# A macaron layer on one core: the order of TensorE's work within a quarter of a head pair, and transposes in tiles of 64

## The reference, cut to what matters

```python
x = x + 0.5 * ffn(layernorm(x))
x = x + attn(layernorm(x))      # 16 heads of 64; inside: softmax(q k^T / 8) v, w_proj, + bias + x, layernorm
x = x + 0.5 * ffn(layernorm(x))

def fp4_linear(x, w):           # blocks of 16 rounded to an FP4 grid, scaled by the block's maximum
    return einsum('bsk,nk->bsn', fp4_quant_dequant(x), fp4_quant_dequant(w))
# ffn: silu(fp4_linear(x, w_gate)) * fp4_linear(x, w_up), then fp4_linear(., w_down); inner width 352
```

## Time and profile before

| | us |
|---|---|
| median of three runs | 2568.18 |
| lowest and highest | 2564.86, 2571.95 |
| the profiled execution's own time | 2570.78 |
| its span, first to last instruction | 2569.0 |
| PE busy | 2312.5 (90%) |
| DVE busy | 1721.6 (67%) |
| POOL busy | 1412.9 (55%) |
| ACT busy | 1202.1 (47%) |

### The profile page before, as it was taken

The page is one execution under the profiler, slowest core; times in us unless marked ns, Lnnn a source line. Parts: engine busy times, 40 slices in busy tenths (PEclk is TensorE's granted clock), DMA queues, the critical chain, the costliest instruction groups (busy, mean ns, idle before and its releaser), DMA issues.

```text
span 2569.0 us, 45690 instructions
## 1 busy us (share of the span) xinstructions
PE 2312.5 (90%) x16292; PEld 1220.1 (47%) x16292; DVE 1721.6 (67%) x2830; ACT 1202.1 (47%) x1813; POOL 1412.9 (55%) x1323
## 2 busy tenths in 40 slices
PE   3799899999999999999989998999999999999984
PEld 1344444545454454545444454454545455454542
DVE  4465677767677776767667676776767677765643
ACT  1345454545545454544545444454454545444431
POOL 2255555656556565556556555565655656555551
PEclk7799999999999999999999999999999999999985
DMA  1000000000000000000000000000000000000000
GB/s 49 5 6 2 3 5 6 6 2 10 3 6 6 2 10 2 10 2 6 6 3 10 2 10 3 6 6 2 10 3 6 6 2 10 2 6 2 6 2 9
DMA packets 167394, 16.40 MB, mean 6 GB/s; under 512 B 148160, under 2 KB 166784, under 8 KB 167168
## 3 DMA queue, kind: packets, MB, share of 16 engines
q1 hardware_dynamic: 167168, 13.39, 4.5%
HBM read 7.03 MB, written 4.19 MB: 4 GB/s over the span
## 4 chain that ended last, share of the span: by engine, by line
PE 67%; DVE 20%; issue 6%; ACT 6%; POOL 1%; DVEq 0%; DMA 0%; SPq 0%; ACTq 0%; POOLq 0%
PE pS L943 16%; PE pO L970 12%; PE pM L927 8%; DVE nmax L779 7%; PE pX L991 5%; PE pM L1085 5%; PE pX L955 4%; PE pM L980 3%; PE FpF L284 2%; PE LpF L284 2%; PE FpF L295 2%; PE LpF L256 2%; PE LpF L267 1%; DVE QL L901 1%; PE FpF L256 1%
## 5 line engine op out<-in xcount | busy, mean ns | idle before, releaser
L646 POOL TENSOR_TENSOR ES<-ES,E 128x512 f32<-128x512 f32 x512 | 693.4, 1375 | 265.1 <-ACT E L731 263.5
L779 DVE TENSOR_REDUCE nmax<-pX 128x2 fp32r<-128x1024 f32 x512 | 622.1, 1215 | 161.2 <-PE pX L955 158.3
L731 ACT ACTIVATE E<-pS 128x1024 f32<-128x1024 f32 x512 | 523.2, 1022 | 420.4 <-PE pS L943 408.7
L970 PE MATMUL pO<-E,VA 128*64 128x512 f32 x2048 | 554.6, 620 | 0.0
L640 POOL TENSOR_TENSOR ES<-E 128x512 f32<-128x512 f32 x256 | 320.5, 1274 | 366.0 <-ACT E L731 366.0
L943 PE MATMUL pS<-QH,KH 64*128 64x512 f32 x1024 | 258.7, 501 | 19.6 <-issue 15.1
L927 PE MATMUL pM<-xf,w_raw 128*64 128x512 f32 x1024 | 268.1, 600 | 3.1 <-DVE QL L901 2.4
L741 ACT ACTIVATE KH<-pM 128x512 fp32r<-128x512 f32 x128 | 76.6, 598 | 358.2 <-PE pM L927 358.2
L955 PE MATMUL pX<-KH,QH 64*128 64x512 f32 x1024 | 233.2, 405 | 4.2 <-DVE nmax L779 2.7
L943 PEld LDWEIGHTS pS<-QH,KH 64*128 64x128 f32 x1024 | 96.8, 185 | 285.2 <-issue 253.8
L991 PE MATMUL pX<-wp,ON 128*64 128x128 f32 x2048 | 141.6, 280 | 98.9 <-DVE nmax L779 79.3
(11 more groups left out here) (141 smaller groups left out, 3402.0 us busy)
## 6 DMA issues: line engine op xcount, KB each, us to landing
RROW<-RC SPq DMA_DIRECT2D x512, 2.0 KB, 2.0
xin<-in_L_attn_x SPq DMA_DIRECT2D x16, 256.0 KB, 2.8
SH<-nmax SPq DMA_DIRECT2D x256, 2.0 KB, 2.0
LC<-LROW SPq DMA_DIRECT2D x256, 2.0 KB, 2.1
out<-X SPq DMA_DIRECT2D x16, 256.0 KB, 2.3
w_raw<-in_L_attn_w_q SPq DMA_DIRECT2D x1, 512.0 KB, 4.0
w_raw<-in_L_attn_w_k SPq DMA_DIRECT2D x1, 512.0 KB, 5.6
w_raw<-in_L_attn_w_v SPq DMA_DIRECT2D x1, 512.0 KB, 6.7
```

Source lines behind the costliest of these rows:

```text
L646: ins = g.tensor_tensor(ES[par][:, hd, :], ES[par][:, hd, :], E[s][:, hd, :], ALU.add)
L731: a.activation(E[s][:, :, :], pS[:, :, :], ACT.Exp).then_inc(s_exp, 1)
L779: v.tensor_reduce(nmax[px % 2][:, :, t:t + 1], pX[:, :, :], AX.X, ALU.max, negate=True).then_inc(s_max, 1)
L970: ins = pe_.matmul(pO[half(hd), :], VA[of][:, kt, j * 128 + 64 * hd:j * 128 + 64 * hd + 64], E[kt][:, hd, :], start=kt == 0, stop=kt == KT ...
```

## The change

In PE's walk three things are moved. The product for the maxima comes ahead of the scores in quarters 0, 1 and 3, and stays behind them in quarter 2. The projection goes from before the K product to the end of quarter 1, behind the FFN work; the V product of quarter 3 also goes behind the FFN work. On DVE the sum into Yacc goes behind the remainders QL and KL of its quarter. The last piece of the transposes of h has 64 columns: it starts at column 288 instead of 320, so columns 288 to 319 are turned twice, and the down product takes 128 rows of every chunk. The rows of its weights that meet the doubled columns are zero: w_down's last 32 columns are loaded by a DMA of their own, 32 places on.

```diff
@@ pe_h
-                f0 = ch * 128 + 64 * n
-                w = min(64, FF - f0)
-                ins = self.nc.tensor.matmul(self.pF[64 * n:64 * n + w, ch * 128:(ch + 1) * 128], row[:, f0:f0 + w],
+                f0 = min(ch * 128 + 64 * n, FF - 64)
+                ins = self.nc.tensor.matmul(self.pF[half(n), ch * 128:(ch + 1) * 128], row[:, f0:f0 + 64],
@@ pe_down
-                rows = min(128, FF - ch * 128)
-                                                self.hqT[0:rows, ch, t * 128 + 64 * n:t * 128 + 64 * n + 64],
-                                                self.wdT[0:rows, ch, :], start=ch == 0, stop=ch == FT - 1)
+                                                self.hqT[:, ch, t * 128 + 64 * n:t * 128 + 64 * n + 64],
+                                                self.wdT[:, ch, :], start=ch == 0, stop=ch == FT - 1)
@@ SP, setup (and DVE waits for s_wraw 96 instead of 80)
-                sp.dma_start(wraw[:, 2, 0:FF], w_down).then_inc(s_wraw, 16)
+                sp.dma_start(wraw[:, 2, 0:FF - 32], w_down[:, 0:FF - 32]).then_inc(s_wraw, 16)
+                sp.dma_start(wraw[:, 2, FF:FP], w_down[:, FF - 32:FF]).then_inc(s_wraw, 16)
@@ DVE, body: behind QL (s == 0) and KL (s == 1) instead of ahead of them
+                        if s == 1 and there(i - 3, NP):
...
+                            v.tensor_tensor(Yacc[yp][:, :], pX[:, 0, :], Yacc[yp][:, :], ALU.add).then_inc(s_yacc, 1)
@@ PE, a new helper
+                def max_round(i, p, s):
+                    if s < 2:
+                        for_maxima(i + 1, p + 1, s + 2)
+                    else:
+                        for_maxima(i + 2, p + 2, s - 2)
@@ PE, body
                     for s in range(KT):
+                        if s != 2:
+                            max_round(i, p, s)
                         if there(i, NP):
                             scores(i, p, s)
...
-                        if s < 2:
-                            for_maxima(i + 1, p + 1, s + 2)
-                        else:
-                            for_maxima(i + 2, p + 2, s - 2)
+                        if s == 2:
+                            max_round(i, p, s)
...
-                        if s == 1 and there(i - 3, NP):
-                            project(i, p)
                         if s == 1 and there(i + 2, NP):
                             pe.wait_ge(s_qlo, i + 3)
                             per_head(1, p2, x).then_inc(s_k, 1)
                         if s == 2 and there(i - 1, NP):
                             row_sums(i - 1, 1 - p % 2)
+                        first_ffn(b, 4 * p + s, bpar)
+                        last_ffn(b, 4 * p + s, bpar)
+                        if s == 1 and there(i - 3, NP):
+                            project(i, p)
                         if s == 3:
                             for r in rounds_at(i):
...
-                        first_ffn(b, 4 * p + s, bpar)
-                        last_ffn(b, 4 * p + s, bpar)
```

More of the change, by code:

```diff
@@ L768, in _ @@
                 v.memset(LROW[:, :], 1.0).then_inc(s_ones, 1)
-                dve.wait_ge(s_wraw, 80)
+                dve.wait_ge(s_wraw, 96)
                 F.qh.maxima(nc, dve, 0, F.h[:, 0:NW], slice(0, NW // BLK))
@@ L906, in body @@
                                                    ALU.mult, ALU.subtract).then_inc(s_klo, 1)
+                        if s == 1 and there(i - 3, NP):
+                            bo, yp = (b, bpar) if p >= 3 else (b - 1, 1 - bpar)
+                            dve.wait_ge(s_proj, i - 2)
+                            dve.wait_ge(s_y0, bo + 1)
+                            wait(dve, s_yacc, i - 3)
+                            v.tensor_tensor(Yacc[yp][:, :], pX[:, 0, :], Yacc[yp][:, :], ALU.add).then_inc(s_yacc, 1)
                         first_ffn(b, t, bpar)
```

## The result

The changed kernel took 2473.1 us (median of 4 runs, 2470.86 to 2474.6) against 2566.5 us for the kernel before in the same runs (2560.94 to 2571.95): ratio 0.9635, 95% interval 0.9612 to 0.9659. The forecast was 2473. The profiled execution has a span of 2469.1 us against 2569.0.

A forecast was written before the change was run, and what follows sets the result against it. PE was taken to bound most of a batch, VectorE near it in the third and fifth pair. Terms -116 + 20 - 14 + 10 - 43 + 8 + 46 + 0.5, with clock -6, gave -95 and 2473 us; range 2405 to 2545.

The forecast's parts named there:

- the new waits: Waits added by moving the projection: 12 us for Yacc in quarter 2, 8 us for quarter 3's leading product; 20 us.
- B: V product behind quarter 3's FFN work: -14 us of its wait for ON, +10 us at the next pair's leading product.
- A: Projection last in quarter 1, behind the K product, which covers its wait for VectorE's reduction: -116 us.
- under 20: Sign that the forecast is right: under 20 us of idle time before the projection.
- The 8 us in quarter 3: Quarter 3's leading product waits some 0.5 us for the reduction where VectorE has FFN work behind Yacc, first pair.
- D: Product for the maxima ahead of the scores in quarters 0, 1, 3: strided load exposed, 0.12 us 384 times, +46 us.
- The 35 us that I left in the third pair: V product's wait for ON in the third pair, expected to stay: 15 x 2.3 = 35 us.
- C: Transposes of h in 64-wide pieces: 0.75 instead of 1.09 us, 128 times, -43 us; 8 given back where VectorE paces.
- Rival 4: The strided load of the product for the maxima is hidden in the change of mode: 2427 us, chance 0.12.
- Clock: Steady part: up to 24 us lie in short stretches at 1.2 GHz; with fewer PE waits, -6 us.
- the gate (1): Rival: leading product for the maxima waits for a late reduction and holds up scores behind; slower, chance 0.07.
- VectorE as the bound (2): Rival: VectorE takes over in four pairs, only fourth, sixth, seventh and eighth gain; -53, 2515 us, chance 0.14.

The follow-up runs named there:

- e6: Changed kernel with the projection ahead of the K product again and the sum into Yacc ahead of QL and KL: 2533.3 us, ratio 0.9849.
- e10: Kernel before with only the product for the maxima put ahead of the scores in quarters 0, 1 and 3: 2582.3 us, ratio 1.0054.
- e7: Changed kernel with the V product ahead of the FFN work of quarter 3 again: 2489.7 us, ratio 0.9673 to the kernel before.
- e2: Changed kernel with the scores ahead of the product for the maxima in all four quarters: 2435.7 us, ratio 0.9482 to the kernel before.
- e9: Kernel before with only projection, V product and sum into Yacc moved; scores leading, old 32-wide transposes: 2485.0 us, ratio 0.9676.
- e8: Changed kernel with the 32-wide last transpose piece, 96-row chunk and single w_down load again: 2537.2 us, ratio 0.9855 to the kernel before.
- e1: Kernel before with only the 64-wide transposes, 128-row down product and split weight load: 2558.3 us, ratio 0.9961.
- e3: Changed kernel, product for the maxima loading 128 consecutive QH columns instead of every fourth: 2437.7 us, ratio 0.9489 to the kernel before.
- e4: Changed kernel with VectorE's moments of the layernorm after attention, and GpSimd's root, one quarter later: 2436.5 us, ratio 0.9487 to the kernel before.

## Why the prediction was right

The sum came out at -95 us and the measurement at -94. The mechanisms were the forecast ones, the sizes were not all: the transposes brought 15 us more, the new waits cost about 16 more, the projection gained about 13 less and of the +10 of B only 4 came. That the total is right to 1 us is luck; the terms as the traces have them add up to -84, and 7 us of the rest are waits that the sum did not name: the scores' for the exponentials, 4.5 us before and none after, and the turn of the hardware loop, 15.1 and 12.1.

**A, -116, with +20 of new waits.** Right in kind. The projection's idle fell by 87 us, to 12.3, within the "under 20" that I had asked for, though not to 5; from the starts its loss fell from 119 us, which the sum had right at 121, to 16. A visit now runs as forecast. PE and VectorE in quarter 1 of the sixth pair, against the earlier trace rows:

```profile
1200.81 1.08 PE L976 MATMUL pO<-E,VA 128*64 128x512 f32 x4
1201.72 1.03 PE L926 MATMUL pM<-xf,w_raw 128*64 128x512 f32 x4
1202.58 1.04 PE L997 MATMUL pX<-wp,ON 128*64 128x128 f32 x16
```
```profile
1201.11 1.16 DVE L778 TENSOR_REDUCE nmax<-pX 128x2 fp32r<-128x1024 f32 x1
1203.43 0.69 DVE L898 SCALAR_TENSOR_TENSOR KL<-pM,KH 128x512 fp32r<-128x512 f32 x1 [1.15 <-ACT KH L740]
1204.04 0.68 DVE L905 TENSOR_TENSOR Yacc<-pX,Yacc 128x512 f32<-128x512 f32 x1
```

The next group starts 0.91 after times_v, the K product covers the reduction, and Yacc follows KL. The new wait for Yacc showed itself otherwise than I had put it. It is no idle time of the matmul: the wait sits on its weight load. In quarter 2 of the next visit Yacc ran from 1219.45 for 0.69 us, the load started at 1220.21, and the matmul at 1220.37, half under the scores, half exposed:

```profile
1220.21 0.34 PEld L954 LDWEIGHTS pX<-KH,QH 64*128 64x128 f32 x2
1220.37 0.49 PE L954 MATMUL pX<-KH,QH 64*128 64x512 f32 x2
1220.79 1.08 PE L976 MATMUL pO<-E,VA 128*64 128x512 f32 x4
```

From the starts in the trace, the load begins 0.07 us after the end of Yacc in all of the 123 visits that the trace has whole, and times_v comes late in all of them: by 0.10 us in 76, by 0.20 in 12 and by 0.45 in 35. That is 26 us, nearly all of which no idle column shows. Of the 35, 30 are the fifth and the sixth pair of each batch, two of my three pairs without FFN work in quarter 1, where KL has to be done first; the extra 0.35 us makes 12 us, as forecast. The 0.10 in every visit I had missed. The 8 us in quarter 3 are there too, 0.52 us once a batch, in the fifth pair and not in the first. With 12.3 - 2.7 = 10 us of visible waits for reductions the new waits are some 36, against my 20. A and D were not independent, as e6 and e10 showed: lead and move cover the same 0.48 us. In a sum over the whole change that does no harm; taken one by one my terms would have failed.

**B, -14 and +10.** The forecast net, -4, is too near to e7's 10 for its interval to tell them apart. From the starts V's loss fell from 49 us, as the sum had it, to 39, so 10 instead of 14; and the leading product behind V comes 0.05 to 0.09 us late in 47 visits, 4 us instead of 10. The 35 us that I left in the third pair are there, 35.4 in all pairs together. PE in that pair:

```profile
1155.48 1.08 PE L976 MATMUL pO<-E,VA 128*64 128x512 f32 x4
1158.82 1.08 PE L1093 MATMUL pM<-w_raw,xf 128*64 128x512 f32 x4 [2.25 <-DVE ON L887]
1159.86 0.62 PE L954 MATMUL pX<-KH,QH 64*128 64x512 f32 x2
```

2.25 us of idle time, as before (2.11), because the run of VectorE starts only after Yacc.

**C, -43, 8 given back.** Too small for the place where it stands and much too large for C alone: -50 on top of the moves (e2 against e9), -57 inside the change (e8), -10 on the old order (e1). The step that was mis-sized is "six pairs at 0.11 and one change of mode": for half of the transposes no change of mode is left, 0.43 us each. My 8 us back for VectorE belonged to the old order, where e1 gave back 15 in waits and some 17 in clock. In front of the scores the 0.75 us of the sum is what the trace has. The down product kept its time, as I had taken: 2.72 us to the next start with 128 rows, 2.74 with 96.

**D, +46.** Right: e2 measured 39, e3 37, and the trace has the leading matmul at 0.62 us. From the starts, a leading product of the maxima holds PE 0.46 us and a leading score product 0.34, 0.12 x 384 = 46; e2 and e3 show less because waits and clock took some back. Rival 4, the hidden load, is refuted by e3: the trace's load times decide over the rule of the Trainium skill (TensorE: Matmul & The Clock Gate, LDWEIGHTS), by which both loads cost the same for their 128 columns.

**Clock, -6.** In the steady part 27 us at 1.2 GHz instead of 44, a gain of about 8. It is a number of single executions: e8, with the same V waits as the changed kernel, had 58.

Of the rivals, the gate (1) is real and small, 22 us in e10 and 10 in the change; VectorE as the bound (2) holds for neither pair. The fifth stood at 16.4 us, yet e2 has it at 15.3 with the same work for VectorE; the third fell from 20.9 to 18.5 in e4, so it was bound by the place of 3 us of work, not by its amount.

## What to carry to other kernels

Wait, load and clock are three prices of one order on a matrix engine. A product that must wait for its buffer should have independent work in front of it, not behind it; the first product after a change of mode should be the one with the cheapest stationary load; and pieces in one mode belong side by side. An edit that only shortens the engine's work can be worth a quarter of its size in one order (e1: 10 of 42 us) and all of it in another (50 of 49), so remove the long waits first and measure the edit again.

## What the runs showed of the hardware that I had not expected

- Less work for PE can go with a lower clock: with 42 us of work removed and V's waits grown from 2.11 to 2.46 us, the time at the 1.2 GHz level went from 44 to 78 us (e1); which of the two did it no run separates. With the 2.25 us waits removed it went from 27 to 14 (e4), and all four stretches left there stand at gaps of 2.2 to 2.4 us in PE's work at the turn of the hardware loop.
- A weight load read with a stride of four elements takes 305 ns for 128 columns, a plain one 183 (e3).
- A change between the modes 128\*64 and 64\*128 adds 0.10 us behind a transpose of h in the changed kernel: 0.76 us to the start of a product in the other mode, 0.66 to one in the same.
- A wait can cost time without any idle time of the matmul, when it holds back only the weight load: 0.10 us a visit. With the plain load of e3 the load begins as late and the 0.10 us are gone.
